# An attention pipeline in eleven steps: the order of the work inside a step is changed on four engines

## The reference

```
h = tok_embed(x) with cls_tok ahead                     # [32, 37, 256]
h = h + attn(layernorm(h))                              # 4 heads, causal softmax, plus a linear-attention
                                                        # memory read (elu(q)+1) @ mem / ((elu(q)+1) @ z), mixed by
                                                        # sigmoid(betas); output projection Wo, bo
h = h + moe(layernorm(h))                               # shared MLP 256->1024->256 (silu) on every token, and
                                                        # the best 2 of 8 experts of the same size, softmax gates
```

## Time and profile before

| what | value |
|---|---|
| three runs | 346.59, 346.70, 347.11 us, median 346.7 |
| the profiled execution | 347.21 us, span of the instructions 345.4 us |
| PE busy | 319.7 us (93%) |
| DVE, ACT, POOL busy | 223.5, 186.9, 150.1 us |
| granted TensorE clock, mean | 0.978 of full |

### The profile page before, as it was taken

How to read it: one execution, slowest core, us unless ns; L and a number is a source line. 1 busy time by engine, 2 the same in 40 slices (tenths; PEclk the granted TensorE clock), 3 DMA queues, 4 the chain that set the end, 5 groups by cost and what they waited for, 6 DMA issues and landing times.

```text
span 345.4 us, 9654 instructions
## 1 busy us (share of the span) xinstructions
PE 319.7 (93%) x3378; PEld 269.7 (78%) x3378; DVE 223.5 (65%) x497; ACT 186.9 (54%) x407; POOL 150.1 (43%) x224
## 2 busy tenths in 40 slices
PE   7798789999998899799999999999999999999970
PEld 6577678888887698699999777777777877777850
DVE  0235677898878778789988678675655555554530
ACT  1147557778778687666677878762323232323220
POOL 0525556666775234510172154455536353543330
PEclk9989999999999899999999999999999999999995
DMA  7583333324322000491479778233232232323121
GB/s 243 152 266 125 103 102 108 119 80 151 90 85 92 26 27 26 88 347 34 90 197 278 271 217 229 49 63 62 36 60 41 54 47 50 47 47 47 17 32 15
DMA packets 18612, 36.36 MB, mean 105 GB/s; under 512 B 3301, under 2 KB 10952, under 8 KB 18568
## 3 DMA queue, kind: packets, MB, share of 16 engines
q1 hardware_dynamic: 12136, 27.71, 25.2%
q0 software_dynamic: 6432, 8.03, 15.1%
HBM read 28.52 MB, written 7.21 MB: 103 GB/s over the span
## 4 chain that ended last, share of the span: by engine, by line
PE 80%; DVE 8%; POOL 3%; issue 3%; ACT 3%; DMA 1%; SPq 0%; DVEq 0%; ACTq 0%; POOLq 0%
PE bank L744 20%; PE bank L757 13%; PE bank L467 9%; PE bank L557 6%; PE bank L759 6%; PE bank L598 6%; PE bank L492 5%; PE bank L500 3%; PE bank L510 2%; PE bank L546 2%; PE bank L424 2%; PE bank L514 1%; PE bank L668 1%; DVE weights L1207 1%; DVE weights L1216 1%
## 5 line engine op out<-in xcount | busy, mean ns | idle before, releaser
L744 PEld LDWEIGHTS bank<-x_t,weights 128*128 x1248 | 87.4, 98 | 25.6
L744 PE MATMUL bank<-x_t,weights 128*128 128x128 f16 x1248 | 103.9, 219 | 0.0
L920 ACT ACTIVATE act_out<-bank 128x512 f32<-128x512 f32 (+2 forms) x72 | 42.1, 585 | 88.2 <-PE bank L744 75.9
L757 PE MATMUL bank<-weights,hid_hi 128*128 x192 | 73.3, 382 | 0.5
L1143 POOL DMA_INDIRECT out_rows<-y,add_id x26 | 41.7, 1606 | 71.0 <-DVE y L1443 52.7
L1261 DVE SCALAR_TENSOR_TENSOR hid_lo<-act_out,hid_hi 128x512 f16<-128x512 f32 (+2 forms) x72 | 48.6, 680 | 13.1 <-ACT hid_hi L931 11.6
L759 PE MATMUL bank<-weights,hid_lo 128*128 x192 | 52.3, 273 | 0.0
L1267 DVE SCALAR_TENSOR_TENSOR weights<-stage,weights 128x1024 f16<-128x1024 f32 x36 | 42.9, 1216 | 0.4 <-ACT weights L884 0.2
L1070 POOL TENSOR_SCALAR weights<-weights 111x1 f32<-111x1 f32 x22 | 14.4, 655 | 57.1 <-DVE weights L1169 57.0
L884 ACT ACTIVATE weights<-stage 128x1024 f16<-128x1024 f32 x36 | 36.8, 1047 | 0.0
L467 PE MATMUL bank<-weights 128*111 128x256 f32 x132 | 34.1, 411 | 2.3 <-ACT weights L832 1.0
(11 more groups left out here) (142 smaller groups left out, 548.7 us busy)
## 6 DMA issues: line engine op xcount, KB each, us to landing
stage<-in_w_ffn SPq DMA_DIRECT2D x36, 512.0 KB
weights<-in_patches SPq DMA_DIRECT2D x11, 333.0 KB, 3.2
x_rows<-rows SPq DMA_DIRECT2D x11, 111.0 KB
out_rows<-weights SPq DMA_DIRECT2D x10, 111.0 KB
out_rows<-y POOLq DMA_DIRECT2D x9, 119.0 KB, 5.8
weights<-in_w_embed SPq DMA_DIRECT2D x3, 256.0 KB, 4.7
weights<-in_w_qk SPq DMA_DIRECT2D x1, 512.0 KB, 5.8
slot_rows<-x_rows,gather_id POOLq DMA_INDIRECT x26, 3.8
```

Of the source, the lines that this page charges most:

```text
L744: mm = nc.tensor.matmul(o, weights[:, bass.ds(base + 2 * k * CHUNK + 2 * (col - col % D) + w * D + col % D, P)], x_t[:, b, (2 * x + k) * P ...
L757: nc.tensor.matmul(bank[5 + b][0:m, :], hid_hi[:, b, c * P:c * P + m], weights[:, bass.ds(at, 2 * D)], start=(c == 0), stop=False)
L920: nc.scalar.activation(d_, s_, ACT.Silu, scale=1.0 / (X_SCALE * W_SCALE)).then_inc(hid_acted, 1)
```

## The change

The stages and their arithmetic stay as they are. Each of PE, ACT, POOL and DVE gets another order inside a step. On PE the step was turn_prob, turn_xln, turn_attn, scores, embed, project, mix_values, turn_rows, project_out, logits. It becomes turn_prob, logits (of the tile one step older), project, turn_attn, scores, embed, mix_values, turn_rows, project_out, and turn_xln of the newer tile, which is now at the end of step s where it was near the beginning of step s + 1. ACT, POOL and DVE are put in an order that goes with it. In the list behind the loop one logits call is added on PE (it was in the loop), and on DVE max_score(NT - 1) comes after finish_sq(NT - 1) and top2(NT - 5).

```
--- before.py
+++ after.py
@@ -607,32 +607,28 @@
                 nc.tensor.matmul(bank[7][0:T, 0:T], ones[:], ones[:], start=True, stop=True)
 
             for s in range(NT + 1):
+                if s == 0:
+                    embed(0)
                 if 0 <= s - 3:
                     turn_prob(s - 3)
+                if 0 <= s - 6:
+                    logits(s - 6)
                 if 0 <= s - 1:
-                    turn_xln(s - 1)
+                    project(s - 1)
                 if 0 <= s - 4:
                     turn_attn(s - 4)
                 if 0 <= s - 2:
                     scores(s - 2)
-                if s == 0:
-                    embed(0)
-                if s + 1 < NT and s != 1:
-                    embed(s + 1)
-                if 0 <= s - 1:
-                    project(s - 1)
-                if s == 1:
+                if s + 1 < NT:
                     embed(s + 1)
                 if 0 <= s - 3:
                     mix_values(s - 3)
-                if s < NT and 0 <= s - 5:
+                if 0 <= s - 5:
                     turn_rows(s - 5)
                 if 0 <= s - 4:
                     project_out(s - 4)
-                if s == NT:
-                    turn_rows(s - 5)
-                if 0 <= s - 5:
-                    logits(s - 5)
+                if s < NT:
+                    turn_xln(s)
 
             def ranks():
                 pe.wait_ge(members_ready, 1)
@@ -673,6 +669,7 @@
                     mm.then_inc(y_ready, 1)
 
             turn_prob(NT - 2)
+            logits(NT - 5)
             turn_attn(NT - 3)
             scores(NT - 1)
             project_out(NT - 3)
@@ -941,28 +938,26 @@
                     nc.scalar.mul(gate_pair[:, :, 0], s_wg, W_SCALE).then_inc(gate_hi, 1)
                 if 0 <= s - 3:
                     copy_prob_t(s - 3)
-                if 0 <= s - 1:
-                    copy_xln_t(s - 1)
-                if 0 <= s - 4:
-                    copy_attn_t(s - 4)
                 for c in chunks_at(s):
                     split_hi(c)
-                if 0 <= s - 2:
-                    exps(s - 2)
-                if s < NT and 0 <= s - 5:
-                    norm2(s - 5)
                 if s < NT:
                     norm1(s)
                 if 0 <= s - 1:
                     copy_qkv(s - 1)
-                if s == NT:
+                if 0 <= s - 4:
+                    copy_attn_t(s - 4)
+                if 0 <= s - 5:
                     norm2(s - 5)
+                if 0 <= s - 2:
+                    exps(s - 2)
                 if 0 <= s - 1:
                     tanh_q(s - 1)
                 if 0 <= s - 5:
                     copy_x2_t(s - 5)
                 if 0 <= s - 6:
                     tanh_gap(s - 6)
+                if s < NT:
+                    copy_xln_t(s)
 
             def copy_x_t(j):
                 act.wait_ge(x_turned, j + 1)
@@ -1089,17 +1084,17 @@
             nc.gpsimd.memset(silu_warm[:], 0.0).then_inc(half_ready, 1)
             nc.gpsimd.memset(y[:, 2], 0.0).then_inc(dummy_zero, 1)
             for s in range(STEPS):
-                for t in ((0, 1) if s == 0 else (s + 1,)):
-                    if t < NT:
-                        inv_std(t, stats1, rstd1, t % 2, 1.0)
-                if 0 <= s - 1 < NT:
-                    relu_q(s - 1)
+                if s == 0:
+                    inv_std(0, stats1, rstd1, 0, 1.0)
+                    pool.wait_ge(out_bias_in, 16)
                 if s < NT:
-                    if s == 0:
-                        pool.wait_ge(out_bias_in, 16)
                     pool.wait_ge(xln_ready, s + 1)
                     nc.gpsimd.tensor_tensor(h[0:T, s % RING], h[0:T, s % RING], s_ob[0:T],
                                             ALU.add).then_inc(h_bo_ready, 1)
+                if 0 <= s - 1 < NT:
+                    relu_q(s - 1)
+                if s + 1 < NT:
+                    inv_std(s + 1, stats1, rstd1, (s + 1) % 2, 1.0)
                 if 0 <= s - 4 < NT:
                     inv_std(s - 4, stats2, rstd2, 2 + s % 2, X_SCALE)
 
@@ -1281,23 +1276,23 @@
                     nc.vector.scalar_tensor_tensor(out=gate_pair[:, :, 1], in0=s_wg, scalar=W_SCALE,
                                                    in1=gate_pair[:, :, 0], op0=ALU.mult,
                                                    op1=ALU.subtract).then_inc(gate_pair_ready, 1)
-                if 0 <= s - 2:
-                    max_score(s - 2)
-                    finish_sq(s - 2)
                 if s == 0:
                     embed_h(0)
-                if s + 1 < NT:
-                    embed_h(s + 1)
+                if 0 <= s - 6:
+                    top2(s - 6)
+                if 0 <= s - 2:
+                    finish_sq(s - 2)
+                    max_score(s - 2)
                 if 0 <= s - 5:
                     row_lo(s - 5)
                 for c in chunks_at(s):
                     split_lo(c)
+                if s + 1 < NT:
+                    embed_h(s + 1)
                 if 0 <= s - 3:
                     combine(s - 3)
                 if 0 <= s - 4:
                     residual(s - 4)
-                if 0 <= s - 5 and s < NT:
-                    top2(s - 5)
 
             def over(ap, *dims):
                 return ap.broadcast_to([T, *dims])
@@ -1467,9 +1462,9 @@
             def shared_lo(n, half_):
                 split_hidden(n, n % 2, tokens_of(n), half_)
 
-            max_score(NT - 1)
             finish_sq(NT - 1)
             top2(NT - 5)
+            max_score(NT - 1)
             residual(NT - 3)
             row_lo(NT - 4)
             combine(NT - 2)
```

More of the change, by code:

```diff
@@ L943, in _ @@
                     copy_prob_t(s - 3)
[L944 to L947, removed]
                 for c in chunks_at(s):
                     split_hi(c)
[L950 to L953, removed]
                 if s < NT:
```

4 lines of the change are left out of this document (2 added, 2 removed).

## The result

The changed kernel takes 349.83 us (median of 20 runs, 346.62 to 351.45), the kernel before 346.66 (median of 20 runs, 344.77 to 347.83). The ratio is 1.0084, with a 95% interval of 1.0063 to 1.0106: slower by 0.84%, 2.9 us. The profiled execution took 349.30 us, its span is 347.5. The runs of the changed kernel are spread widely: three of 20 lie at 346.6 to 347.0 with a mean granted clock of 0.980 or 0.981, the rest at 349.0 to 351.5 with 0.969 to 0.977.

A forecast was written before the change was run, and what follows sets the result against it. PE, 80% of the chain, was taken as the bound. Terms: -3.55 (up to s = 10) + 2.45 (s = 10 and 11) + 1.0 (list) + 2.0 (clock) = +1.9 on 346.7, so 348.6 us; range 345.3 to 350.6.

The forecast's parts named there:

- falls that don't come: In the list, the old kernel's clock fall after its waits would be avoided: 0.5 us taken off the clock's price.
- The stall of turn_attn goes: In each full step, PE's wait at turn_attn for combine disappears: -0.43 us, from 9.99 to 9.56 before hand-overs.
- the 0.1 charged for hand-overs: In s = 6 to 9, hand-overs that just fit add 0.1 us to 9.56, giving 9.65 per step.
- s = 10 starts 3.55 us earlier: Up to the start of s = 10: shorter early and full steps bring it to 96.4 from 99.95, -3.55 us.
- mix_values without cover idles 2.4 us in s = 10 and 11: Without embed, PE waits about 2.4 us for exps in each; steps take 9.55 and 9.4 us instead of 8.67 and 7.82.
- The loop through residual, inv_std, norm2 and exps: Across steps, norm2 ahead of exps makes a loop of 9.4 to 9.55 us that sets s = 10 and 11.
- The list: exps(10) hangs on DVE's finish_sq and top2: Behind the loop, DVE work before max_score(10) puts exps(10) at 120.75 instead of 120.21; list term +1.0 us.
- The clock: Long idle pieces bring half-clock falls of 3 us: 1.3, 0.5 and 0.7, less 0.5, +2.0 us; bounds 0 and 4.0.
- The third fall, ahead of turn_rows(7): In the list, a PE wait of about 1.7 us ahead of turn_rows(7) lowers the clock, priced at 0.7 us.
- Rival A: Across the end of the loop and the list, no clock fall and the lead used up: 346.6 us, chance 0.16.
- Rival B: In the list, the lead survives if exps(10) starts before 119.4: 345.4 us, chance 0.22.
- Rival C: In the steps, POOL colliding with DVE makes the mix-to-exps loop exceed PE's step, 9.9 us each: 350.4 us, chance 0.14.

The follow-up runs named there:

- e7_fill_half: The changed kernel with five unused embed-sized matmuls on PE between scores and mix_values in s = 10 and 11: 346.40 us, ratio 1.0031.
- e10_norm2_tail: The changed kernel with exps ahead of norm2 on ACT in s = 10 and 11 only: 349.45 us, ratio 1.0089.
- e2_max_first: The changed kernel with max_score(10) put back ahead of finish_sq(10) and top2(6) in DVE's list: 348.19 us, ratio 1.0045.
- e8_fill_half_max: The changed kernel with five unused matmuls before mix_values in s = 10 and 11, and max_score(10) first in DVE's list: 344.25 us, ratio 0.9939.
- e5_out_ahead: The changed kernel with project_out and turn_xln ahead of mix_values on PE in s = 10 and 11 only: 346.26 us, ratio 1.0011.
- e3_norm2_late: The changed kernel with exps ahead of norm2 on ACT in all steps, as before: 357.82 us, ratio 1.0307.
- e1_fill_gap: The changed kernel with ten unused embed-sized matmuls on PE between scores and mix_values in s = 10 and 11: 350.43 us, ratio 1.0115.
- e9_norm2_early: e8_fill_half_max with norm2(7) right behind exps(10) on ACT, ahead of the table load and first silu: 345.36 us, ratio 0.9964.
- e6_tail_order: The changed kernel with PE, ACT and DVE reordered in s = 10 and 11 and PE and DVE in the list: 346.69 us, ratio 0.9999.

## Why the prediction was right

The measured 349.83 lies in the range, on the forecast side and 1.2 us above the forecast of 348.6. The cause was in the main the forecast's (the idle pieces and the low clock that comes with them), but that the sum came out this near is in part luck, as errors cancel. Up to s = 10 the lead was 2.8 us and not 3.55; steps 10 and 11 cost 6.15 us, of which the terms had 2.45 and, for the clock, 1.8; the list added nothing, where the terms had 1.0, another 0.7 for the clock, and 0.5 taken off for falls that don't come. From turn_xln(0) to logits(10) that makes +3.4 us against a forecast of +1.9.

- *The stall of turn_attn goes.* Right: no idle there. Full steps were put at 9.65 and took 9.73. Against the 9.56 that the prediction had without hand-overs, project is slower by 0.24 us behind logits than behind embed, which the earlier trace rows could not show, and turn_prob shorter by 0.07; the 0.1 charged for hand-overs does not show as idle.
- *s = 10 starts 3.55 us earlier.* Measured 3.76, but 1.0 of it is the earlier start of that execution, so the lead was 2.8, 0.8 us smaller than laid out: 0.3 in the four full steps, the rest ahead of them (s = 6 started at 59.99 in the trace before, not 59.97, which changes nothing).
- *mix_values without cover idles 2.4 us in s = 10 and 11.* Right, 2.36 twice. With full clock the steps take 9.54 and 9.33 (e7_fill_half), predicted 9.55 and 9.4.
- *The reason given for it was half wrong.* The loop through residual, inv_std, norm2 and exps was said to set these steps. It does not bind (e10_norm2_tail); scores, max and exps alone do. Both led to the same moment: in the profile after max(8) ends at 101.51 and exps starts at 101.55, right behind norm2's second part, so the number came out. That the two paths end together is an accident of this kernel's sizes; the number 9.4 for the loop is not confirmed by it.
- *The list: exps(10) hangs on DVE's finish_sq and top2.* Right in kind: max_score(10) started at 122.59, right behind top2. Its size: 1.1 and 2.1 us by the profiles of e2_max_first and e8_fill_half_max, 1.6 and 2.1 by the medians, predicted as 1.0. But the sum also needed what the kernel before loses in the same list, its own wait of 0.97 us and its own 3.4 us at half clock, and the prediction gave no credit for those: measured from the first turn_prob of the list to turn_rows(7), the change is 0.0 us.
- *The clock.* Right in kind, and by two of three figures too small: +2.0 was said, and e7_fill_half gives back 3.0 us by the measure and 3.4 by the medians, 1.8 by the ratios. It stood in steps 10 and 11, which took 3.8 us longer than with the clock full; the prediction had put 1.3 and 0.5 there. One reason is the second fall, which lasted 6.8 us in the profile after where the forecast reckoned with 3 for each; why it lasted so long there, and 3.4 in e10_norm2_tail, is open. The third fall, ahead of turn_rows(7), did not come in this execution; it did in e5_out_ahead. The Trainium skill, TensorE: Matmul & The Clock Gate, section What's actually happening, says that full clock is released by activity and not the default. The trace agrees: in steps 10 and 11 each fall to 0.50 came with an idle piece of 2.36 us, and no fall came in the profiles where the pieces were filled.
- *Rival A* (no fall of the clock, 346.6) is what e7_fill_half brings about, 346.4 by the median and 347.7 by its ratio. *Rival B* (345.4) needs exps(10) before 119.4; it came at 123.3. *Rival C* (steps of 9.9): not seen; POOL's inv_std stayed undisturbed in the full steps (its first instruction took 0.22 or 0.23 us).

## What to carry to other kernels

In a pipeline written out by hand, ask of each wait which piece of work stands in it, and then whether that piece exists in the first and last steps too. A new order that is better in every full step (here by 0.27 us) can lose more in two steps at the end (here 6.15 us, against 2.8 us won by then). Where a change makes PE stand still in one long piece instead of several short ones, reckon with half the clock for the work behind it; filling the piece with matmuls for nobody is a cheap test, if the filling is sized to the piece, and here it was even part of the fastest version. When the kernel before has waits and low clock of its own in a part, they belong in the sum too.

## What the runs showed of the hardware that had not been expected

- The clock fell to half at each of the eight idle pieces of 2.36 us in four profiles (after, e2_max_first, e3_norm2_late, e10_norm2_tail), for about 3.4 us five times and 6.8 us three times (worked out from the mean clock in slices of 1 us or less). The longer fall came at the second piece in two of these profiles and at the first in one. After the last wait of 1.63 us the clock stayed full in six profiles, with the 0.8 us wait ahead of it too (e1_fill_gap, e7_fill_half), and fell in one, e5_out_ahead. Five dummy matmuls in each piece, 2.4 us, kept it at 1.00 there in the three profiles that have them (e7_fill_half, e8_fill_half_max, e9_norm2_early); the mean clock of four of the 12 runs of e7_fill_half says that it fell somewhere in those.
- One execution differs from the next in part by where and how long the clock falls: the same changed kernel gave 346.6 and 351.5 us, and e6_tail_order 344.2 and 347.5, the fast ends with the higher mean clock. The mean is not all of it: 349.30 and 351.29 us both have 0.973. It also counts the last 5 to 10 us of the kernel, at half clock in every profile, in which PE has nothing to do.
- Sixteen float32 matmul instructions of 128x111 (project's q and k) take 1.77 us behind embed, 1.87 behind turn_prob alone (s = 3 to 5) and 1.94 behind logits, with the same data and clock. Why was not tried.
